# Two hand-written orders of one fused attention kernel: key and value weights on another DMA queue, all five engines' orders replaced

## The chip, the cores and the metric

The kernel runs on one core of a Trainium2 chip. The core has five engines that run side by side: TensorE (PE in the profile, with PEld for its weight loads), VectorE (DVE), ScalarE (ACT), GpSimd (POOL) and SyncE (SP), which here only issues DMAs. ScalarE issues DMAs on a queue of its own too. The metric is the time of one execution in microseconds on the device, the median of three runs.

## The reference

Thirty-two sequences `x` of 64 tokens with 256 features attend to a context `ctx` of the same shape, in four blocks, one after the other; everything is float32:

```
x = L0(x, ctx)   # whole-slab normalisation, 8 heads of 64 channels attending over the 256 feature columns, residual
x = L1(x, ctx)   # layer norm of the context, 16 heads of 16, key mask, gated (tanh) residual
x = L2(ctx, x)   # queries from x, keys and values from context and x together, key mask, RMS norm, MLP of 1024, residual
x = L3(x, ctx)   # self attention, cross attention, MLP of 1024, each behind a layer norm, with residuals
```

All four need softmax over masked scores. The weights are loaded once; activations of a pair of sequences stay on the chip from the first block to the last.

## The kernel before, in words

The 32 sequences are worked on as 16 pairs (a pair fills the 128 partitions). The work on a pair is cut into stages, each with a letter: `n` normalises `x` for L0 and makes its values from the context, `q` its queries, `a` scores and softmax (eight units of two 512-column score banks), `d` transposes the probabilities, multiplies them with the values and adds the residual; `k` does what depends on the context alone (keys and values of L1, L2 and L3's cross attention); `b` is L1, `e` L2's attention, `g` L2's MLP, `c` L3's self attention, `f` its cross attention, `h` its MLP. `s` is the setup (weights loaded and combined once), `w` are matmuls without use on a constant tile, `y` is the store.

For each stage and pair there is a Python generator for each engine that takes part, such as `act_n(i)` or `pe_a(i)`; it issues a few instructions between two `yield`s. What an engine issues next is set by a string in `ORDER`, one letter for one step of that stage's generator, which `weave` (line 207) walks through. So each engine is strictly in order, stages of several pairs are interleaved, and what is not fixed by the strings is done by semaphores: an instruction waits for what it reads and for the buffer that it writes. PSUM is used as seven rotating banks; `BANK` says which bank each fill takes, and an eighth bank (`attended`) collects the output of `d`, and of the `w` matmuls. A planner outside the program wrote `ORDER` and `BANK` from costs that it gives to each step.

The setup on PE (`pe_s`, line 1261) has seven steps: transpose the query and key weights of L0 (line 1268, its copy out of PSUM is line 1327 on VectorE); multiply them into one matrix per head ("m", lines 1276 and 1279; it waits for the two loads `cols` and `bv_raw`, which share one semaphore); multiply value and output weights ("wvo", line 1286); a bias ("bias", line 1293); three rows of bias (line 1301). The first `WARM_UP` of the `w` matmuls (line 1235) stand at the start, the rest near the end, behind the last pair's L0 residual.

The first steps of PE and SyncE, decoded from the strings (a number is the pair; x00, x01: transposed probabilities; att: attended matmuls; v0, v1 of `n`: line 433; q: line 510; a: line 539; k1: line 659):

```
PE: w x13, wT, n0.mean, k0.cT, m, wvo, bias, k0.nT, n0.var, n0.v0, k0.k1, q0 q0, a0.0, n0.v1, a0.1, k0.v1, k0.k2, row1,
    k0.v2, d0.x00, a0.2, a0.3, n1.mean, ...
SP: x of pair 0, context of pair 0 for k, cols+bv, context of pair 0 for a (cc), q0+o0 of wb, rows, residual, context of pair 1 for k,
    q1+o1, x of pair 1 (waits for q0), w1+w2, masks, ...
```

ScalarE issues seven setup loads first (`act_s`, line 1308): two halves of L0's query and key weights, its value and output weights, and three 512 KB loads of key and value weights (kv0 and kv1 of `wb`, kv1 of `wc`).

Of the kernel before, what the change touches and what calls it, by code (L numbers as in the profile page):

```python
# [62 lines left out]
WARM_UP = 13  # L63
IDLE_WORK = 62
# [18 lines left out]
def transpose_fills():  # L83
    fills = []
    for u, j, n in units():
# [24 lines left out]
        "nksnssdksnsebssnfsndnkebbndfnknfnedenybbbkfndnkydenkebdnfbnyffdnnyebyeknkbednfnynkkdbddnefenyfnkyyfbnedfnykbkn"  # L110
        "enbfykebdnenbdefkynffydyyy"),
    "pe": (
        "wwwwwwwwwwwwwsnksssknnkqqanakkskdaanddkdddaadddsdnsddaddddaqddqaadkdddkkddnanaddbkbdndbdddaaddbdbddbaabkeddnee"
        "dededdddddqqaaddeekbeennaedbekkbagndddggggddbdbaabdcdbcecncecdddaacdeecdddcdcedqqafddddfddfeeeennaefddfebfbkkf"
        "kaagkdggndggbdddkhkkchcckbchhbhacbdddnbaddaedcedcedacdecedddfdddfqqfddeebeeannefbefafdkfdkkaagkkgghkkdgnghdkhd"
        "dbaddchncdchdbbccabdddbdaaeccedcdeceeddqqfdddfdfddeeeenanebffafekkkbfaagkkgdghgdgkknhhbdhdchckccbbddacbnddddba"
        "ddaaecceecdddcdeeddfddddfqqfddeeeebnanefbefaaafgkgkkfgkdkggbdkhnkdhchdcckbchhddacddbddbnddaaacdbcdedcedeceeddf"
        "dddfdqfddeebeeqanebfefanafdkkfkadnkgkkggbdhgghhkbcdhcccbhddcaabddkdbndcddecdaaceeddcdeeqddfdddfdddfeeeeqnaneff"
        "afbebkkfkaadkgkkdgngkhgddgkbddchhccchhacbddbddnbaddcbddecaacdeedceeddqdfdddfddfeeeebaqnanefbfafekkdkfddkgdnkgg"
        "ggbddaadhdkkckdccdhbcnhbddcabdhdbchecaacedecdeedddfdddfqfddeeeennqaefbfefbkfkkaaagkdghghdnhbdgngkkkkhchcdcbcbd"  # L120
        "dcabddddbaddecdecdaacedcededdfdddfdqfddeeeenqaeffnafekkabkfbdkkgkdggbadgdgkhnddbkchchdcbchhacbdddnbaddaaecceed"
        "ddcdeceqdddfdddfddfeeeeaqnneaffebfbkkkfagkdgdghdggbadkhhcnkbcchbhccddbkddaadbdckcneddaacdeeecdddeqdddfdddfddfe"
        "eeenqanebffeafbkfkgkdaadgkgdghngbdhkcnhckccddcabdkddhbhdbckddaaacbceddeecddeeddqfddddfddfeeeebnaqebffeanfdkdkf"
        "gaakgngkggdbhdkkhchbcccddcdnbdhaabhkddbkcceddaaceddedcdeeddfddddfqqddfebeeebnaefnfefkkfkaaagkkgdghkgkhdgbdhdkc"
        "hccchcddbbdaabdccddbcddecdaaefdefdfdeedddddfdfdfkkkfdkebekbeewbehkehhgbbgbgbgegeeewwweckcchcwwwwwwwceeeehecwec"
        "wwwckgcggfggfwwfwwwwcwwwcccffcwfkfwwwcwwwcwwwcwhchwwfhfwwfhhwfwwfwwwfwwwwfwwwwwwwwwwhwwwhhhh"),
# [12 lines left out]
    "dve": (
        "nknsnknknnsksnsnnnsnknananaaknassaaandaadnakknnaaaadanadsannkenbaakdndaasaaakadaadanaaandnaaankdndbbbbnbanbbaa"  # L140
        "bndbdbbabaaabaabaanaennedndaeeneeeeddaeaedaekbanaennaaeaegagggkbgnbbbnknadbdgagbkbbfgcbbabbcencaacbdbaacnancec"
        "cdccaccaacnccnccebncadaacndcffaefeeefeeaddfaeffefafefenffnffeffdfkaeagkgfngggafaakhgnahdgdaahnbegcbbccnnhcbbbb"
        "bnabhbkbcbkhckhafcaccbddncacaacbccacaadcennccneaaackdncafffeefeedefdkefffedefefefaffafeffnfeagaagfkngfagbghane"
        "hahkanhdgaggnhcccdahckbknbbnabkabnadbbcncbbdbnbhbkakccccancbccanbccadcacfcanceedcffaaafeeeafeeedfdffeffffeefef"
        "ndnfffefaakefagagafgggaafhkahahaghgandngcnkbhncnchcnbbdbbbbbcbakbhcbbbaccccbaddcbcaacaccenaccacaenneanacdacndf"
        "fefeafeeeddfekkeefffdkefffefaffaenffegagfaggangaakfafhggbkhaahnhngbbbakcbccbencbnhbbbdhnbbdkafccbhacncaccdcdcc"
        "akncaakbcncaacbcadaanncenedacffefeafeeedfkedffedfffeeeffaaffebnfaefgafkaggnngafnafagnhkhaaknhafghdbbgbbbbgbcnb"
        "chbccbhebcdacnbcchaccaccbdacacdnabcccncnaanaknaaeckeacdkffdefaeefeeedkdfeffefeffefffaffnffadeaaanfkaegggnfgaag"
        "afanbahhgdhkhgkndgccbccbbbkbabbbnbhnbcbbhnchaccccadcdkccacabnabcaneccnacadkaaecaedncafnfefeeefkededfedfbefeffe"
        "faafffnnfefaffaakfeaggaggnngdfankgndegagbhhchbnccbabhcabdabkaacbfbnbdkbahbcnhbcnccncaccbckancbacdhcccaanaaceea"  # L150
        "cffkfdafeeeeeedfdeffkefedfffefnffffefankafegagbgnfnhghaahgakahaaaghdnnnghbnbgbcbcckekbcbbabbcnbfdkchbabccackcc"
        "bdncadcbackabnaccnccaenadaceaacfaffdeeafeeedfedfffefeefefffafnffekdfanegggafgaafghkaaadekggfbbnhbbbbhnbhdbgncc"
        "ccnbaakbabchhncabnhaccccbandcdbaaaccckaacaccecnannekdnacdacfkeefafeefededfeeffeffefdafffanfeffnfaaegakgfggabgn"
        "afkhahhhgdgegbbbbcccnbbdcfbhnhcbcabbkbnanbahcccccacccbcacandaabccdnaakanknaaacaneneabcffddeekfeefeeddfefffefef"
        "dnffefafeffakefngaggafggkefhanahaahagankdghnnagcnaccnbcbbbbbdhbckbfbcnhcccbcnbnabcdcaccdcccahcbaakaabnacnaaeae"
        "dcfadfefeefeebeddfeefdfffefefaafffefkfkefgaagggnnkafgnkfnaahhaahngghadnkagcbbbcbeckbcbhnbdbbhbacbbncccccancadn"
        "ccabhcnabcadcckcfanaacnaeaaedcfdkafbfeefeeedkefdeedffefeefefkffffefffaeaggfknngfagaagkahahhaghgakaahgccbbcdacb"
        "bhkkbbdbcecbbbbcchckccbcccacabdcccbadacfbacfaffaafeaadefaffffakdfeffeffeffdfekefdeedeekeefhehhbbhbbebbeggegbgb"
        "gbkhbbbgbgbgceccfecheeeeeceeceececececccccecccecgggggcckffhfgfggfcccffcfffffcfcffffccccfcccfcccchcfhhhccffffhh"
        "ffffffffffffhfffhhhhhhh"),  # L160
# [99 lines left out]
def build(nc, dram, out):  # L260
    ctx = ExitStack()
    with ctx:
# [20 lines left out]
        wb = sb("wb", [P, WCOLS])  # L283
        wc = sb("wc", [P, WCOLS])
# [1075 lines left out]
        def sp_s():  # L1360
            sp = nc.sync
# [185 lines left out]
```

## Time and profile before

| | us |
|---|---|
| median of three runs (1220.17 to 1222.36) | 1220.33 |
| the profiled execution | 1221.77 |
| its span, from the first to the last instruction | 1220.0 |
| PE busy | 1189.9 |
| DVE busy | 958.0 |
| ACT busy | 848.0 |
| POOL busy | 614.0 |

A span is shorter than its execution's time by what lies before the first and after the last instruction, here 1.77 us. In the rows below, a line such as L539 is that line of the kernel; `out<-in` are the program's tile names; `x26` counts instructions (a float32 matmul is two of them); PEclk is the granted clock of TensorE, 1.00 for 2.4 GHz and 0.50 for 1.2 GHz.

### The profile page before, as it was taken

The page shows a single profiled execution, that of the slowest core. Times are in us where ns is not written, and L with a number is a line of the kernel's source. Part 1 is how long each engine was busy: PE and PEld are TensorE (multiplying, and loading weights), DVE is VectorE, ACT ScalarE, POOL GpSimd, SP SyncE. Part 2 cuts the span into 40 slices and gives each one's busy share as a digit, 9 for nine tenths or more (in the row PEclk, how much of TensorE's full clock was granted, in tenths as well). Part 3 has the DMA queues.
Part 4 walks back from the last instruction along what each step waited for, and adds up shares of the span by engine and source line. Part 5 has one row for each costly group of instructions (what it writes and reads, how often), then busy time and mean ns, then how long its engine had stood idle before and what let it go on. Part 6 is the DMA issues. An engine that isn't in the chain of part 4 may idle for free.

```text
span 1220.0 us, 35295 instructions
## 1 busy us (share of the span) xinstructions
PE 1189.9 (98%) x13174; PEld 974.5 (80%) x13174; DVE 958.0 (79%) x2298; ACT 848.0 (70%) x2275; POOL 614.0 (50%) x1003
## 2 busy tenths in 40 slices
PE   8999999999999999999999999999999999999998
PEld 7778787787887878788787887878787787877877
DVE  3778886969788797787969788697887969789764
ACT  2877676787867668686776667677686777866543
POOL 2653663637455473644646456373654645363341
PEclk7999999999999999999999999999999999999999
DMA  6501000000000000010100100000000000000000
GB/s 207 192 3 28 2 27 2 16 20 25 15 6 12 22 14 12 12 30 1 29 15 2 32 2 20 17 16 2 25 12 17 24 8 16 2 12 2 2 6 10
DMA packets 27623, 27.91 MB, mean 23 GB/s; under 512 B 11072, under 2 KB 25408, under 8 KB 26816
## 3 DMA queue, kind: packets, MB, share of 16 engines
q1 hardware_dynamic: 25808, 23.42, 6.3%
q10 hardware_dynamic: 1648, 2.23, 0.6%
q8 instruction: 109, 1.79, 0.6%
q14 instruction: 58, 0.48, 0.1%
HBM read 23.53 MB, written 2.10 MB: 21 GB/s over the span
## 4 chain that ended last, share of the span: by engine, by line
PE 75%; DVE 11%; issue 4%; POOL 4%; ACT 4%; DMA 1%; SPq 0%; POOLq 0%; DVEq 0%; ACTq 0%
PE bank L932 9%; PE bank L659 9%; PE bank L942 8%; PE bank L539 7%; PE attended L614 7%; PE bank L599 7%; PE bank L665 5%; PE bank L694 4%; PE bank L720 4%; PE bank L683 3%; PE bank L707 3%; PE bank L652 2%; PE bank L510 2%; ACT p_a L575 2%; DVE nmax_a L554 2%
## 5 line engine op out<-in xcount | busy, mean ns | idle before, releaser
L586 POOL TENSOR_SCALAR p_a<-p_a,rec_a 128x256 f32<-128x256 f32 x512 | 248.6, 502 | 116.3 <-DVE rec_a L560 116.3
L575 ACT ACTIVATE p_a<-bank,nmax_a 128x256 f32<-128x256 f32 x512 | 237.9, 475 | 57.3 <-DVE nmax_a L554 55.8
L554 DVE TENSOR_REDUCE nmax_a<-bank 128x2 f32<-128x512 f32 x256 | 170.7, 680 | 25.7 <-PE bank L539 25.3
L599 PE MATMUL bank<-ident,p_a 128*128 128x128 f32 x1024 | 143.7, 275 | 2.6 <-POOL p_a L586 1.4
L539 PE MATMUL bank<-cc,q_a 64*128 64x256 f32 x1024 | 133.9, 392 | 1.5 <-DVE p_a L632 0.3
L599 PEld LDWEIGHTS bank<-ident,p_a 128*128 128x128 f32 x1024 | 115.8, 141 | 19.6 <-issue 11.8
L614 PE MATMUL attended<-p_a,v_a 128*64 128x256 f32 x1024 | 125.2, 386 | 0.1
L539 PEld LDWEIGHTS bank<-cc,q_a 64*128 64x128 f32 x1024 | 93.6, 186 | 32.4 <-issue 19.4
L575 ACT ACTIVATION_READ_ACCUMULATOR p_a<-bank,nmax_a 128x1 f32 x512 | 105.1, 205 | 0.0
L614 PEld LDWEIGHTS attended<-p_a,v_a 128*64 128x64 f32 x1024 | 67.0, 136 | 44.0 <-issue 12.0
L632 DVE COPY p_a<-bank 128x512 f32<-128x512 f32 x128 | 86.4, 680 | 8.0 <-PE bank L599 7.9
L647 ACT ACTIVATE p_a<-bank 128x512 f32<-128x512 f32 x128 | 75.5, 600 | 15.5 <-PE bank L599 14.7
L932 PE MATMUL bank<-h_xnT,wc 128*128 128x128 f32 x512 | 62.0, 276 | 0.2 <-ACT h_xnT L887 0.2
L932 PE MATMUL bank<-g_xnT,wb 128*128 128x128 f32 x512 | 61.7, 276 | 0.0
L932 PEld LDWEIGHTS bank<-h_xnT,wc 128*128 128x128 f32 x512 | 59.7, 192 | 1.1 <-ACT h_xnT L887 0.7
L932 PEld LDWEIGHTS bank<-g_xnT,wb 128*128 128x128 f32 x512 | 59.5, 192 | 1.0 <-ACT g_xnT L887 0.4
L942 PE MATMUL bank<-wc,h_hid 128*128 128x256 f32 x256 | 59.8, 380 | 0.0
L942 PE MATMUL bank<-wb,g_hid 128*128 128x256 f32 x256 | 59.5, 380 | 0.0
L522 ACT ACTIVATE q_a<-bank,bq 128x512 f32<-128x512 f32 x64 | 41.9, 689 | 23.7 <-PE bank L510 23.6
L1116 POOL TENSOR_TENSOR e_p<-e_p,e_max 128x1024 f32<-128x1024 f32 x26 | 49.1, 1903 | 13.0 <-DVE e_max L749 12.7
L813 POOL TENSOR_TENSOR c_p<-c_p,self_add 128x512 f32<-128x512 f32 x32 | 40.4, 1273 | 23.2 <-DVE c_p L1150 23.2
L813 POOL TENSOR_TENSOR f_p<-f_p,m_add 128x512 f32<-128x512 f32 x32 | 40.5, 1274 | 22.9 <-DVE f_p L1199 22.9
(265 smaller groups left out, 2890.6 us busy)
## 6 DMA issues: line engine op xcount, KB each, us to landing
xx<-in_x SPq DMA_DIRECT2D x32, 128.0 KB, 2.8
cc<-in_ctx SPq DMA_DIRECT2D x32, 128.0 KB, 2.9
wc<-in_wc SPq DMA_DIRECT2D x3, 1024.0 KB, 11.5
k_c<-in_ctx SPq DMA_DIRECT2D x16, 128.0 KB
res_a<-in_x SPq DMA_DIRECT2D x16, 128.0 KB, 2.3
wb<-in_wb SPq DMA_DIRECT2D x2, 1024.0 KB, 6.2
out<-y_out SPq DMA_DIRECT2D x16, 128.0 KB, 2.2
wb<-in_wb ACTq DMA_DIRECT2D x2, 512.0 KB, 6.6
```

What stands on the lines that cost most here:

```text
L539: ins = mm(bs[e][:, qt * D:(qt + 1) * D], q_a[rows_, j, n, qt * P:(qt + 1) * P], cc[rows_, z, n, :], start=True, stop=True)
L554: dve.tensor_reduce(nmax_a[:, n, e, :], ps[:, :].rearrange("p (q k) -> p q k", q=KT), AX.X, ALU.max, negate=True).then_inc(A.s["max"], 1)
L575: last = act.activation(p_a[:, j % 2, n, e, qt, :], ps[:, qt * D:(qt + 1) * D], ACT.Exp, bias=nmax_a[:, n, e, qt:qt + 1], accum_out=sum_a[ ...
L586: last = pool.tensor_scalar(p_a[:, j % 2, n, e, qt, :], p_a[:, j % 2, n, e, qt, :], rec_a[:, n, e, qt:qt + 1], 1.0, ALU.mult, ALU.mult)
L599: last = nc.tensor.transpose(ps[:, kt * D + qt * P:kt * D + (qt + 1) * P], p_a[:, j % 2, n, e, qt, kt * P:(kt + 1) * P], ident[:, :])
L614: last = mm(attended_bank[n * S:(n + 1) * S, 0:D], v_a[:, n, kt, h * S:(h + 1) * S], p_a[:, j % 2, n, e, kt, :], start=h == 0 and kt == 0, ...
L632: release(A, dve.tensor_copy(p_a[:, j % 2, n, 1, :, :], ps[:, :].rearrange("p (k q) -> p k q", k=KT)), i, ("x", u, 1))
L647: release(A, act.activation(p_a[:, j % 2, n, 0, :, :], ps[:, :].rearrange("p (k q) -> p k q", k=KT), ACT.Copy), i, ("x", u, 0))
L659: last = mm(ps[:, m * P:(m + 1) * P], w[:, k, m * P:(m + 1) * P], srcT[:, k, :], start=k == 0, stop=k == KT - 1)
L813: pool.tensor_tensor(v, v, bc(mask_add[:, :], 1, HB), ALU.add).then_inc(T.s["madd"], 1)
L932: last = mm(ps[:, m * P:(m + 1) * P], W["w1"][:, k, cols_], T.xnT[:, k, :], start=k == 0, stop=k == KT - 1)
L942: last = mm(ps[:, 0:D], T.hid[:, m, :], W["w2"][:, m, :], start=m == 0, stop=m == MT - 1)
```

## The change

Three 512 KB weight loads leave ScalarE's setup and become three steps of SyncE's, right behind `cols` and `bv_raw` in the generator. `WARM_UP` goes from 13 to 17, `IDLE_WORK` from 62 to 63. `ORDER` and `BANK` are replaced for all engines; in the planner that wrote them, VectorE and GpSimd were taken to exclude each other. Apart from the `w` matmuls and the three loads, each engine's string holds as many steps of every stage as before.

```diff
-WARM_UP = 13
-IDLE_WORK = 62
+WARM_UP = 17
+IDLE_WORK = 63
...
     "sp": (
-        "nksnssdksnsebssnfsndnkebbndfnknfnedenybbbkfndnkydenkebdnfbnyffdnnyebyeknkbednfnynkkdbddnefenyfnkyyfbnedfnykbkn"
...
+        "nkssebsnsssnsnksdfkssdennsdnbbkdefndnnnebynkfnfybkbedenbkfdydnnfkdeyenbfnyknfdnbkynenefnddfykebknybbnnfeekfbny"
...
     "pe": (
-        "wwwwwwwwwwwwwsnksssknnkqqanakkskdaanddkdddaadddsdnsddaddddaqddqaadkdddkkddnanaddbkbdndbdddaaddbdbddbaabkeddnee"
...
+        "wwwwwwwwwwwwwwwwskwnsnksqqnanakkksaadskddkdnddadnsddsdaddaaddddqddqaaddkdkdkddnanabddkbddbdddnaaddbdbddbaanbdd"
...
     "act": (
-        "skknsqqqaankaaqdaadaakaaddaaadadaqqaqqadadkkakanaabdnabdadbabdabbaabaaedakdaeddqqqeaeaeqebeenaaneadbakggdgbbaa"
...
+        "skkqqqqnsaakaandaadaakaddaaaaddaqaaqqqaaddkaaknkaabnadbdadbabdabbabaaaekdadaedqqdqeaeaebeeenqaaendbaagdbggbkaa"
...
     "dve": (
-        "nknsnknknnsksnsnnnsnknananaaknassaaandaadnakknnaaaadanadsannkenbaakdndaasaaakadaadanaaandnaaankdndbbbbnbanbbaa"
...
+        "nsnkknknnnknsnnnnsnanankakaansssaasadaadnabnnanaknsaddkaaansnaaannddkaaaakeaakddaaadnaaannaanadkdbbbbbbanbaabd"
...
     "pool": (
-        "ssknaaaakakaaaankaaaakaaaaaaaaaaabbaaaaenaaeaaeeakeeaaagagcabacbaekcccaanaagcceaffaaaeefkfeeaaffkgaahakhccbkba"
...
+        "ssknkaaaaakaaanaaaaakakaaaaaaaaaabbaaaneaeaaaaeeekagaekaagaacbcabacancacaeaacceaffaaaeekffeeaagffkgahkaakhccbca"
...
         def act_s():
...
-            load_weights(nc.scalar, wb, "kv0", "b_kv0")
-            load_weights(nc.scalar, wb, "kv1", "b_kv1")
-            load_weights(nc.scalar, wc, "kv1", "c_kv1")
...
         def sp_s():
...
                 sp.dma_start(dst, src).then_inc(setup["cols_in"], 16)
+            yield
+            load_weights(sp, wb, "kv0", "b_kv0")
+            yield
+            load_weights(sp, wb, "kv1", "b_kv1")
+            yield
+            load_weights(sp, wc, "kv1", "c_kv1")
             yield
             load_weights(sp, wb, "q0", "b_q0")
```

Decoded, the new strings start so:

```
PE: w x16, wT, k0.cT, w, n0.mean, m, n0.var, k0.nT, wvo, q0 q0, n0.v0, a0.0, n0.v1, a0.1, k0.k1, k0.v1, k0.k2, bias,
    a0.2, a0.3, d0.x00, row1, k0.v2, ...
SP: x of pair 0, context of pair 0 for k, cols+bv, kv0 of wb, four mask loads, kv1 of wb, context of pair 0 for a (cc), kv1 of wc,
    q0+o0, rows, x of pair 1 (waits for q0), q1+o1, contexts of pair 1, w1+w2, residual, ...
ACT: seven loads become four; k0.cT, k0.xnT, four q0, n0.v0, tanh, first exponentials, ...
DVE: statistics of x, copy of wT, second half of the statistics, context statistics, ...
```

## Rows read from the trace of the kernel before

**Rows 1.** The page's busy table: us, share of the span, instructions.

```profile
PE 1189.9 (98%) x13174; PEld 974.5 (80%) x13174; DVE 958.0 (79%) x2298; ACT 848.0 (70%) x2275; POOL 614.0 (50%) x1003
```

**Rows 2.** Windows: stretch, us, busy of PE/PEld/DVE/ACT/POOL, clock, DMA share, GB/s.

```profile
6.54:10.08 3.54, 1.23 (x10) 0.78 (x8) 2.58 (x12) 0.38 (x1) 0.46 (x1) 0.95 1.06 333
10.08:23.36 13.28, 13.28 (x104) 11.28 (x106) 5.11 (x19) 1.50 (x4) 0.83 (x2) 0.50 0.64 212
...
100.00:1100.00 1000.00, 985.24 (x11134) 806.22 (x11132) 807.04 (x1951) 727.72 (x1960) 529.91 (x855) 1.00 0.05 15
1100.00:1220.00 120.00, 109.30 (x1228) 93.95 (x1224) 83.37 (x179) 57.76 (x115) 37.90 (x54) 1.00 0.02 5
...
24.52:60.80 36.28, 35.71 (x266) 27.08 (x268) 27.36 (x69) 29.16 (x101) 20.38 (x40) 1.00 0.57 199
...
0.00:10.00 10.00, 6.72 (x34) 6.28 (x34) 2.58 (x12) 1.67 (x2) 4.31 (x18) 0.99 0.80 210
```

**Rows 3.** Chain of waits, first 130 us: start us, us, what.

```profile
3.62 6.42 DMA bv_raw<-in_bv
...
11.54 3.60 PE bank L1286 x16
15.14 1.80 PE bank L1293 x32
...
17.77 2.01 PE bank L433 x8
19.78 2.00 PE bank L659 x8
21.79 2.71 PE bank L510 x8
...
24.52 1.13 PE bank L539 x8
25.66 0.86 PE bank L433 x8
...
28.45 0.89 PE bank L659 x8
...
94.45 1.92 PE bank L510 x8
```

**Rows 4.** Timeline, 0 to 40 us: start us, us, engine, line, operation, tiles.

```profile
1.05 5.65 PE L1235 MATMUL attended<-mean_of_all 128*128 128x128 f32 x26 [1.05 <-POOL minus_half L1241]
...
8.41 0.66 DVE L1327 COPY c_p<-bank 128x512 f32<-128x512 f32 x1
...
18.12 0.71 POOL L498 TENSOR_TENSOR small_a<-small_a,minus_half 128x2 f32<-128x2 f32 x1 [7.91 <-DVE small_a L463]
...
19.39 0.23 DVE L474 TENSOR_SCALAR small_a<-small_a,cols 128x2 f32<-128x2 f32 x1
...
20.13 0.73 DVE L478 TENSOR_SCALAR xx<-xx,small_a 128x256 f32<-128x256 f32 x2
...
20.30 0.20 ACT L1320 ACTIVATE tanh_gate<-gate 128x1 f32<-128x1 f32 x1
...
27.10 2.43 SPq L1438 DMA_DIRECT2D m_raw<-in_mask  x4
```

**Rows 5.** DMA issues, first 24 us: tiles, queue, count, KB each, us to landing.

```profile
e_p<-in_rows SPq DMA_DIRECT2D x1, 640.0 KB, 9.8
...
cc<-in_ctx SPq DMA_DIRECT2D x2, 128.0 KB, 8.2
```

**Rows 6.** Groups of VectorE's instructions: busy us, mean ns, idle before.

```profile
L632 DVE COPY p_a<-bank 128x512 f32<-128x512 f32 x128 | 86.4, 680 | 8.0 <-PE bank L599 7.9
...
L754 DVE TENSOR_TENSOR f_p<-f_p,f_max 128x512 f32<-128x512 f32 x32 | 29.4, 919 | 0.4
...
L754 DVE TENSOR_TENSOR b_p<-b_p,b_max 128x512 f32<-128x512 f32 x32 | 22.0, 686 | 0.4
```

**Rows 7.** One of ScalarE's four groups of table loads (66 in all).

```profile
L959 ACT ACT_TABLE_LOAD x33 | 42.3, 1283 | 0.6
```

More of the change, by code:

```diff
@@ L115 @@
[L115 to L119, printed above, removed]
@@ new lines @@
+        "ekeedededdddddqqaddekbeeenanaedbebadkgkdgdgbggbdddaabndcdbcecenccdddaadceedcddcdcedqqafddddfddfeeeebannebffefd"
+        "kkkfaagkkkgddngkghdghbddckhhdbcccbhacbdddnbaddaaecceedcdddceeddfddddfqqfddeeebeananefbfedfdkkaakgfdkgggndgddba"
+        "dhkdkchncbbdchccabkhdbhekddcdcaaceddecdeeddfdddfdqqfddeeebenaaefnfefbkfkkdaagkkghkdgngdghbdhkchcchcbkbddacbddd"
+        "dnbaddaaeddeccecedcdeddqqfdddfdfddeeebeannebfefaaafgkgkdfkgdknghgkkhddbckkccchhhddacdbbdddnabddcbdcdeaacdeedce"
+        "eddfdddfdqfddeeebeaqnebffeaafdkkkfangkkggbhdgghnhdhcbkcdchcnbcddaabkdddbdkcecddaaceddecddeeddfdddfdqfddeeeenan"
@@ new lines @@
+    "dve": (
+        "nsnkknknnnknsnnnnsnanankakaansssaasadaadnabnnanaknsaddkaaansnaaannddkaaaakeaakddaaadnaaannaanadkdbbbbbbanbaabd"
+        "bdbbnabannabaanabnanaenedadnaeeeeededaaeedeeaknbaaaaenaegbgggbbgdabbbkbggdkbbabbgbanecacncacanfnbnbdkcaanceanc"
+        "cdcccacaacccneccanckdndacancffefaeeefeaeaddfefffdefeffefnaffefffaeakfggggefgbaannaaanhkkhgdnhghgcdhnccbbcbbbbk"
+        "babfhbccbbnkbaknhaccacbcddnacacbcacnacaccacenennaacdacfffdafeeeeededffefffdeefefaanffafkfeffaanegdgkfgagagbfan"
+        "gakgnhaadghcncahbnchbabbcbanbnbbnkhbbbcnbdchfccnccnbaacbdacckccheccnacaaecdaaekcffdaefkefaeeedfdeffffekdefeffe"
+        "afnffefafnekagagfbanfhhggaghnfahaagkgkangdahcbbccbbchbcnnbbcdahbbbebkbancccacbddancbacacccaancadncacaeeacnncff"
+        "kdkafeeefeeedfdefeffdfefaaeffnfefffegfgaagbgangnaaafnkgkfaghhnhhdagkcnackcnhcbbbbcbadfkbkhenbbhbbcbbacccacdcac"
+        "ndcanbacnccbcncanaadaaceedacfffaekefeeedfedfffedefkefaefffafefnffaeaakgggfagafagkahahnhbghgbbnabnfbbgbbcenchnc"
+        "dbhncbbcabcndbhkcncccaaccabcncdnabckndacccaaknacaeaedcfdffaeeafeeedfedfkfeffeefefnffafnffedfanknekfgggagaagfaa"
+        "kadkahhahfanghbdgbbbbbbbgckccbhcnbnbkahcbnbchaccaccdcdacancanbccanekcbnccadckbnaeedacfafaefeeafeeefdffdfafedee"
+        "ffffeanfnfafaefankfeggnggfagnaahkghnhnahgdngdcbbbbbafnbaccndbcakbabbnahcbchdabacncaccdcbcckcaccbcncakaehaaceea"
+        "cdafffeefeeedfedfffeefeffkfnfeffdffeaanekfnkggangggaafahhaakabhgghdnafakgncbbcbacdhbncbbbbbbbncbcnkhcccacbcadc"
+        "bkdccachnaaccncenaaaneaacedacfffdeefaeeedfedffkeffekfeffefffnffaenakdfegagbgaggnakfaaahfggbbhaabbhbhbengncnacn"
+        "bbhdbncbcakhkcbkcbdhkacccacdcdccbacaanbccccaanakbcnenaaeacdffdnefeeafeeefddffedefeffenfaffnafeffafaegagkfggagf"
+        "hnnakghanghhdgnbecbbaccbbnkacadhbbnbccfhnabbbbncccaccaccabdaanccncnbacdhkckaaecaeadcadfffefaeeeeefddeffedeffke"
+        "faaffkffaneffnfaeggggfbgaffnaahnhaannkgdahghkangccbncdbcbnbbbahbbkbbcnnbbchccaccaccccdncdneacbhkaackcaabakcdea"
+        "aeacfdffeekafeeedfedffefdfeefffeffaeffafneggaggfaankgaanffahgnaahghhankdgbcbccebncbbnbnbabbbbhbncchkbdcccaacca"
+        "bccaacbhknddccbnkcacaanncaekdaeacffafdeeeeefeeddfedefffefeffeffkffeffaaegfgkngfngaaaghhaaaakhggahagcbbbccfcbbd"
+        "hbbabbbbhckcbdccccacacccccbaachdecdbkbcakakcfffaafeaaadfekffdfaffeffeffeffefdedekdfeeekeefhehhbbhbbebbefggggbb"
+        "gbebbhhbgbkgbgcececceeeeecceeeccececeeckcccecccecgggggcchgfffgfgcccfcfffffcffcfffffcccccfccccfcchchfhhccffffhf"
+        "ffffhfffffffffhfhhhhhhh"),
@@ new lines @@
+    "pool": (
+        "ssknkaaaaakaaanaaaaakakaaaaaaaaaabbaaaneaeaaaaeeekagaekaagaacbcabacancacaeaacceaffaaeekffeeaagffkgahkaakhccbca"
+        "abaccaenaaaccaaeffaaeegffeekkafafgaakhaacahcnbbaccakcaaccaeaefagfaaeeffeekkffahghaaakcaacbacbaccnaaaegacckeaaf"
+        "afaeekffeefgfakaaahahcackacabcbcanacacakaeeaffaaeeffkkeefagfaghakahcccaabkbanccacacaeaaeaaffaaeeffekeffkgagaaa"
+        "hakhccacaabcbcnaaaaccekeaaffaaeegkfkfeeffaagahakhacancaacbbaaccakeccaaaeffaaeegffeekffkghaaahakacccnaababccaec"
+        "caaaaekaffaaeeffeegffkkgahakaahcacacbbakaccacncaeaaaefafgaaeekfkfeeffaagkaahhaccancaabbccaacacakeaaeffaaeegffe"
+        "eaaffkgakhhaakccanbaacbkccaccaeaaaeaffaaeeffeekkgffaghahkacacbcnbacakcaacacaaeaaefaaagfkffeeffkgahahaakcackcbb"
+        "aaccaccgaaaffaaeaeffaaffkkkhehegbbekgcecccceeccgffccffkcffcchcchffffffhh"),
@@ L186 @@
-    "2351042351042351604253")
+    "01234560125346012536454014503623613463450215064210365426452160345215641620356142504365204365120463546513426025"
+    "61561053260415326043215643251643250160413602451346143641560234154356315643015423560142106120614325061342534502"
+    "34650243162501260260412360241534651346153016530165021320143526430562341056236243621360432510432561045324563210"
+    "43562431032135421563402142051240265314021645365140635124035123463260153462016421650413625041632504321504163025"
@@ new lines @@
+    "14252456123560124325632542650243615024651243051260541206534120650354350413260413264056450164501465310462163016"
+    "53204140610451040506413052643056204132065324036241506312054263015360415320415324016540163254106351602536410264"
+    "10625325360245360214306523501324613025461354631561402356215326415360415364012540125346015216052163416231460250"
+    "23125301425301425630412650143502315406251346051236430463504613520436514026531645031456013241025302653023042160"
+    "34512634510210652361306415302153064326541326504625106345106341502361502361540236432640321546023153146531451602"
@@ new lines @@
+    "53160231501505246105246524126504312316251632510462510465213052413056246052604521603452412615206341520635024651"
+    "20312015243062413024135603240165312654132654013240362140316452014532605461046312546246024605324610563165312503"
+    "46251034625146504635406213521635412605412630415623150316423504162136251360513426056245641023502645126304123604"
+    "12360256023415605625032534620134620135426054126305420160140631254310610621520160654321605430636035210643521064"
+    "20346510246351063510623451062345264315205624301526052652463152406316523651243605142605146203514620351430435016"
@@ L189, in fill_places @@
+    "45302164156213546210435213201435261045312046532046531053416052346105304651320413240132640132645012364502136502"
+    "4163524163502416350216")
 def fill_places():
```

79 lines of the change are left out of this document (19 added, 60 removed).

## The prediction

> **What bounds the kernel now.** I read the busy table first, then the windows, then the chain of waits, and last the timeline of the first 25 us. The busy table says that TensorE (PE) is occupied for 98% of the span [rows 1]; since ends of matmuls are modelled, that alone proves little. The windows split it [rows 2]: in the body, from 100 to 1100 us, PE is idle for 1000 − 985.24 = 14.8 us, so no order of instructions can win more than about 15 us there. In the last 120 us it idles 10.7 us, although idle matmuls ("w") fill holes. The start is worse than its busy digits tell: from 10.08 to 23.36 us PE is busy without a break, but at granted clock 0.50, the 1.2 GHz level. Just before, from 6.54 to 10.08, it worked 1.23 of 3.54 us [rows 2]. The reader is to see the price in the chain: the same eight matmuls of line 659 take 2.00 us in that stretch and 0.89 us later, those of line 433 2.01 and 0.86 us [rows 3]. What ends the hole before it is the landing of the small bv vector, 6.42 us after its issue, at 10.04 [rows 3]. From the first scores (24.52) to 60.80, where the last attended matmuls of pair 0 begin, PE is busy 35.71 of 36.28 us [rows 2], so time won before 24.52 is carried on as long as the softmax engines follow, and the body behind it is bound by PE as well.
>
> All terms are differences against the profiled execution, 1221.77 us (span 1220.0 and 1.77 us around it). The median shown is 1220.33; I subtract from that.
>
> **The change part by part.**
>
> *Warm-up.* Sixteen "w" instead of 13 stand ahead of the first transposition, and one more behind the context's transposition. Each is two passes; 26 passes take 5.65 us from 1.05 on [rows 4]. The eight added ones cost 0.9 us at 0.11 us a pass (0.89 us for eight of the same 128x128 shape [rows 3]). They lie in the hole between 6.7 and 10.08 us, whose cover is the wait for bv, so I price them at 0; without that cover they would cost 0.9 us. The first transposition then ends near 7.6 us, and VectorE's 0.66 us copy of it [rows 4], which the new order puts ahead of the statistics' second half, ends near 8.6. So the mean matmul comes near 9, not 8.64, still ahead of bv.
>
> *Weights moved to SyncE's queue.* Three loads leave ScalarE's queue and stand behind cols and bv on SyncE's. Ahead of bv nothing is added; bv may land sooner than 10.04, but PE cannot use it before about 9.0 (the mean above). Bounds 0 and −1.0; I take 0. Behind bv the first attention context (cc) now waits for the issue of two weight loads and four mask loads. The masks took 2.43 us to issue [rows 4], the weights about 0.5 us each, so cc's second issue ends near 8.9 instead of 5.5. By bytes, 2.1 MB stand ahead of it on both queues, which is what 210 GB/s move in 10 us [rows 2]: it lands near 11. If it took its old 8.2 us [rows 5] it would land at 17.1, against a need near 15.6. I take the bytes, 0; the other end is +1.5. The rows load (bias rows) now lies behind more; ScalarE's tanh waits for it and precedes the first exponential. It ran at 20.30 with 6 us in hand [rows 4]. New: by bytes near 17, by its old 9.8 us [rows 5] from an issue near 10.5, 20.3. Need: about 17.5. So 0, other end +2.8. The second weights (w1, w2) and all later loads are freed earlier, since the wait of SyncE for pair 0's query matmuls ends earlier.
>
> *The order up to the first scores.* Old, from 10.08 to 24.52 us: 14.44 us. New, the 1.80 us of bias matmuls (line 1293) and the 2.00 us of the first key projection (line 659) stand behind the scores [rows 3]. That leaves 10.6 us at the old clock. If the clock stays at 2.4 GHz, these shrink: line 1286 3.60 to 1.8, line 433 2.01 to 0.86, line 510 2.71 to 1.92 [rows 3], the setup products 1.46 (10.08 to 11.54) to something between 0.73 and 1.46, the small rest 0.84 to 0.42. Sum 5.7 to 6.5. VectorE's chain to the normalised x then shows: variance, GpSimd's power 0.71, three small steps 0.8 (18.83 to 19.62), normalisation 0.73 [rows 4], about 2.5 us behind the variance matmul, 0.4 us later than line 1286 ends. So the first scores start between 16.2 and 16.9; I take 16.5, 8.0 us earlier. Still owed are bias (0.9 at the full clock) and key projection (0.89): 1.8 us. Net −6.2.
>
> *Body.* The work is the same: each engine's string has the same letters but for "w" and three SyncE loads. On PE the first projection of B follows pair attention more closely, the rest of the handovers stand at like distances; I counted PE work between producer and consumer for each kind and found some shorter and some longer. ScalarE's string changes function tables 68 times instead of 66: 2 x 1.28 us [rows 7], hidden in an engine that is 70% busy; without that cover +2.6. I take 0 for the body; bounds −14.8 (all PE idle gone) and, as the same size upwards, +14.8.
>
> *Tail.* One more idle matmul: 0.2 us, in holes; 0.
>
> Here the Trainium skill speaks against part of the change. Row first: subtracting the maximum takes 686 ns in B and 919 ns in F, with GpSimd at work beside it, but the copy out of PSUM of line 632 stays at 680 ns [rows 6]. The Trainium skill ("SBUF — State Buffer", section "SBUF: two separate sides") says that VectorE and GpSimd lock a shared port pair for whole instructions, but that VectorE takes part only with two SBUF inputs or in a two-port mode. The trace agrees. By the rule, taking the engines to exclude each other altogether keeps apart work that could overlap, so the sum would gain nothing in the body; by the row of F, undoing its stretch gives back 32 x 0.23 = 7.5 us of VectorE's time, if all of it reached PE.
>
> Sum: −6.2 + 0 + 0 = −6.2, so 1214.1 us.
>
> **The rivals.**
> *The clock falls again near 9.7 us.* For it: the small products at 10 us and the waits around them remain. Against: PE now has 0.9 us more of passes, and the context transposition in the hole. Then first scores come at 10.08 + 10.6 = 20.7, 3.8 us earlier; 2.6 us more at half clock cost 1.3, and 1.8 are owed: −0.7, 1219.6 us.
> *The body gains as well.* If half of PE's idle goes because stretches like F's 7.5 us are planned around: −6.2 − 7.4, 1206.7 us. Against it: waits in the body are short and spread over all lines.
> *Slower: results out of PSUM come late.* VectorE runs in order. If the new plan puts one eviction like line 632 (0.68 us [rows 6]) too late on a way for which PE waits, once for each of 16 pairs, that is +10.9: 1220.33 − 6.2 + 10.9 = 1225.0. It decides from 0.54 us a pair (8.6 in all), where the start's gain is used up and 0.2% more. For it: the plan sees exclusion where rows show none. Against: distances on PE are alike.
> *The change doesn't do what it says*: the context still lands late and pushes the first scores by 1.5 us; 1215.6, inside the forecast's own range.
>
> **How the numbers follow.** Forecast (clock stays, body within 3.5 us) 0.50; clock falls 0.22; body gains 0.10; slower 0.18. About 0.2% (2.4 us) is what can be told from no change: faster means below 1217.9, slower above 1222.8. The forecast, 1210.5 to 1217.6, is all faster. The clock rival, spread by 3 us of body, gives a third faster, half the same and the rest slower; the body rival is all faster; the slower rival one third the same. So faster 0.67, same 0.17, slower 0.16. The likeliest case alone: 1210.5 to 1217.6. The range that holds 8 in 10 reaches to the clock rival, most of the body rival and half of the slower one: 1207 to 1223.5.
>
> **What would show it.** Granted clock 1.0 from about 7 to 25 us, line 1286 taking near 1.8 us and the first line 539 near 16.5 us: right. Clock 0.50 in 10 to 23 us: the first rival. Line 433 waiting for cc, or the first exponential for tanh: the load terms were wrong. PE idle in 100 to 1100 us differing from 14.8 by over 4 us, or the body's steps drifting against the old times: the zero for the body was wrong. The work behind pair 0's last attended matmul not coming 6 us earlier though the first scores do: PE did not bind there.

## The result, and the profile after

The changed kernel takes 1199.34 us (median of 4 runs, 1198.61 to 1199.49), the kernel before on the same chip 1220.88 (4 runs, 1220.17 to 1222.36). The ratio is 0.982, 95% interval 0.980 to 0.984. I had forecast 1214.1 and a range of 1207.0 to 1223.5: the direction was right, but the gain of 21.5 us is three and a half times the forecast 6.2, and the time lies below the range.

The profiled execution after took 1199.37 us, span 1197.6. Busy table of the changed kernel:

```profile
PE 1178.5 (98%) x13184; PEld 974.1 (81%) x13184; DVE 942.7 (79%) x2298; ACT 849.1 (71%) x2277; POOL 608.6 (51%) x1003
```

Against [rows 1] VectorE (DVE) is busy 15.3 us less and GpSimd (POOL) 5.4 us less, for the same 2298 and 1003 instructions: they take less time each. The windows of the changed kernel (stretch; us; busy of PE, PEld, DVE, ACT, POOL; clock; DMA share; GB/s):

```profile
6.54:10.08 3.54, 2.10 (x43) 1.83 (x42) 2.48 (x11) 0.38 (x1) 0.23 (x1) 1.00 1.09 277
...
100.00:1100.00 1000.00, 992.53 (x11354) 819.32 (x11352) 812.28 (x1980) 737.49 (x1983) 531.16 (x865) 1.00 0.05 15
1100.00:1197.60 97.60, 90.35 (x979) 78.39 (x978) 60.82 (x143) 45.29 (x86) 30.04 (x41) 1.00 0.02 6
...
11.54:18.36 6.82, 6.82 (x27) 6.07 (x28) 2.36 (x8) 1.99 (x4) 0.23 (x1) 0.50 0.89 274
```

The row 100 to 1100 is the one to read twice. Its busy time rose by 7.3 us against [rows 2], but in the same 1000 us TensorE ran 11354 instructions instead of 11134: 220 more, 2.0%. So busy time alone does not tell how much work a stretch holds.

A mark for the stages is the issue of the last attended matmul (line 614) of a pair of sequences. The view of one line gives the first and last start in a window; here pairs 1 (first row, last start) and 15 (second row, last start), in the kernel before:

```profile
L614 PE MATMUL attended<-p_a,v_a x32: 379/379/430, 90.6 to 100.0; 128*64 128x256 f32 x32
...
L614 PE MATMUL attended<-p_a,v_a x64: 379/379/431, 1075.1 to 1110.3; 128*64 128x256 f32 x64
```

and in the changed kernel:

```profile
L614 PE MATMUL attended<-p_a,v_a x32: 379/379/431, 86.9 to 95.5; 128*64 128x256 f32 x32
...
L614 PE MATMUL attended<-p_a,v_a x48: 379/379/430, 1066.1 to 1088.2; 128*64 128x256 f32 x48
```

So the start gained 100.0 - 95.5 = 4.5 us; the body from pair 1 to pair 15 took 1010.3 us and takes 992.7, 17.6 less, some 1.25 us a pair; what lies behind took 1220.0 - 1110.3 = 109.7 and takes 109.4. Together 22.4 us, the difference of the spans. Between the two marks both kernels run the same number of TensorE instructions (no line's count differs by more than 8), here first before and then after:

```profile
100.00:1110.30 1010.30, 994.63 (x11226) 812.67 (x11222) 817.34 (x1967) 733.32 (x1974) 534.35 (x862) 1.00 0.05 15
```

```profile
95.50:1088.20 992.70, 985.50 (x11226) 813.39 (x11222) 804.50 (x1964) 733.11 (x1975) 529.77 (x862) 1.00 0.05 15
```

Of the 17.6 us, 8.5 were idle time of TensorE (15.7 against 7.2) and 9.1 lay inside its busy time, for 11226 instructions at the same clock. A busy time whose ends are modelled hides part of the waiting.

The start, in the changed kernel's chain of waits:

```profile
2.46 6.09 DMA k_c<-in_ctx
...
11.35 3.19 PE bank L1286 x15
14.54 3.73 PE bank L510 x8
18.27 0.97 PE bank L433 x8
19.24 0.86 PE bank L539 x8
...
21.83 1.09 PE bank L659 x8
...
24.67 1.02 PE bank L1293 x32
```

and its timeline:

```profile
12.61 0.73 DVE L478 TENSOR_SCALAR xx<-xx,small_a 128x256 f32<-128x256 f32 x2
...
18.89 1.21 PE L539 MATMUL bank<-cc,q_a 64*128 64x256 f32 x8
...
20.00 0.21 ACT L1317 ACTIVATE tanh_gate<-gate 128x1 f32<-128x1 f32 x1
```

bv no longer ends the first hole, the context tile k_c does, at 8.55 us. The clock stays at 1.0 until 11.54 (before: 9.70) and is at 0.50, the 1.2 GHz level, until 18.36 (before: 23.36). In that stretch line 510 pays 3.73 us, more than the 2.71 of [rows 3], where the clock came back before its end, and line 1286 3.19 for 15 records against 3.60 for 16; line 659, behind it, pays 1.09 instead of 2.00. First scores: 18.89 us instead of 24.52. The loads that answer to [rows 5], after (count, KB, median us to landing):

```profile
e_p<-in_rows SPq DMA_DIRECT2D x1, 640.0 KB, 6.7
...
cc<-in_ctx SPq DMA_DIRECT2D x4, 128.0 KB, 4.2
```

Two of these four context loads are pair 1's; the two of pair 0 took 4.8 and 5.3 us.

The groups that answer to [rows 6], after:

```profile
L632 DVE COPY p_a<-bank 128x512 f32<-128x512 f32 x128 | 86.3, 679 | 6.2 <-PE bank L599 5.5
L754 DVE TENSOR_TENSOR c_p<-c_p,c_max 128x512 f32<-128x512 f32 x32 | 23.1, 723 | 0.3
...
L754 DVE TENSOR_TENSOR f_p<-f_p,f_max 128x512 f32<-128x512 f32 x32 | 22.1, 690 | 0.5
```

F's subtraction lost nearly all of its stretch (919 to 690 ns; B's 686 is the yardstick), the copy out of PSUM stayed as it was, and C's went down from 781 ns before:

```profile
L754 DVE TENSOR_TENSOR c_p<-c_p,c_max 128x512 f32<-128x512 f32 x32 | 25.0, 781 | 0.4
```

### The profile page after: what moved, and what is told of

It reads as the page before. It is cut to its first block, busy times and chain, and to the rows that moved or that the text cites. A ratio compares the mean times of both kernels' runs of the same rounds, so it can differ in the third digit from the quotient of the medians.

```text
span 1197.6 us, 35319 instructions
## 1 busy us (share of the span) xinstructions
PE 1178.5 (98%) x13184; PEld 974.1 (81%) x13184; DVE 942.7 (79%) x2298; ACT 849.1 (71%) x2277; POOL 608.6 (51%) x1003
## 3 DMA queue, kind: packets, MB, share of 16 engines
q10 hardware_dynamic: 1216, 0.66, 0.3%
## 4 chain that ended last, share of the span: by engine, by line
PE 88%; DVE 4%; issue 3%; POOL 2%; ACT 2%; DMA 1%; SPq 0%; POOLq 0%; DVEq 0%; ACTq 0%
PE bank L659 10%; PE bank L539 9%; PE bank L932 9%; PE attended L614 9%; PE bank L942 9%; PE bank L599 9%; PE bank L694 6%; PE bank L665 5%; PE bank L720 4%; PE bank L683 4%; PE bank L707 4%; PE bank L652 3%; PE bank L510 2%; PE bank L433 2%; PE bank L711 2%
## 5 line engine op out<-in xcount | busy, mean ns | idle before, releaser
L586 POOL TENSOR_SCALAR p_a<-p_a,rec_a 128x256 f32<-128x256 f32 x512 | 245.9, 498 | 93.2 <-DVE rec_a L560 92.7
L942 PEld LDWEIGHTS bank<-wb,g_hid 128*128 128x128 f32 x256 | 47.0, 190 | 5.5
L942 PEld LDWEIGHTS bank<-wc,h_hid 128*128 128x128 f32 x256 | 46.6, 190 | 5.7
```

Of the source, the lines that this page charges most:

```text
L586: last = pool.tensor_scalar(p_a[:, j % 2, n, e, qt, :], p_a[:, j % 2, n, e, qt, :], rec_a[:, n, e, qt:qt + 1], 1.0, ALU.mult, ALU.mult)
L942: last = mm(ps[:, 0:D], T.hid[:, m, :], W["w2"][:, m, :], start=m == 0, stop=m == MT - 1)
```

## The experiments

All ran beside the kernel before (1221.1 to 1221.6 us by the set); medians are given. "Body" is the time between the two marks above.

**Which part of the order brings what.** Splices of the two orders: on every engine one order up to a time early in pair 1, then the other order for what is left. The three weight loads go with the start.

```
-ORDER[e] = old[e]
+ORDER[e] = new[e] up to 60 us + (old[e] without these steps)      # s1, s1b
+ORDER[e] = old[e] up to 63 us + (new[e] without these steps)      # s2
```

> On every engine the changed kernel's order up to 60 us, then the old order of what is left; loads of the key and value weights on SyncE as changed. In the traces the changed kernel leads by 4.1 us (at equal TensorE work) when pair 0's last attended matmuls are issued and by 21.7 us at pair 15's. Theory (the start and the body gain apart from each other): the lead of the start is kept and nothing is added, 1216 to 1217.5 us. Rival (the body gains because the loads and first pairs come earlier): near 1199 to 1204 us. Rival (the start's lead is given back to the softmax engines): 1219 to 1221 us.

> The mirror image: the old order and the old loads up to 63 us, then the changed order of what is left. Theory (the body's order gains 17.6 us by itself): 1203 to 1204.5 us. Rival (the body needs the new start): 1215 to 1221 us.

s1: 1219.87 us, the range of the rival in which the lead is given back. s2: 1207.74, outside both ranges. In both TensorE stood still once at the seam for a bank that exponentials still held (2.1 us in s1, 3.0 in s2), since the banks of one order met the fills of the other; in s2 the granted clock was 0.50 behind it, from 67.1 to 70.5 us. So s1 was repeated with the old body's banks renumbered.

> As s1_new_start_old_body, but the old body's seven banks are renumbered so that those that come free first at the seam are used first. In s1 TensorE stood 2.26 us at 59 us, for a bank that exponentials of the scores still held; up to there it led by 4.9 us. Theory (the lead of the start is kept by the old body): 1216.5 to 1218 us. Rival (the old body gives it back at another place): 1219.5 to 1221 us.

1216.92 us (ratio 0.997, 0.996 to 0.998), the theory's range: the start alone brings 4.4 us and keeps it. The marks of s1b:

```profile
L614 PE MATMUL attended<-p_a,v_a x32: 379/379/430, 86.0 to 95.4; 128*64 128x256 f32 x32
...
L614 PE MATMUL attended<-p_a,v_a x64: 379/379/430, 1070.5 to 1105.6; 128*64 128x256 f32 x64
```

and of s2:

```profile
L614 PE MATMUL attended<-p_a,v_a x32: 379/379/430, 95.2 to 103.7; 128*64 128x256 f32 x32
...
L614 PE MATMUL attended<-p_a,v_a x64: 379/379/431, 1059.8 to 1096.2; 128*64 128x256 f32 x64
```

Body 1010.2 us with the old order and 992.5 with the new, whatever start stands ahead of it. The 17.6 us belong to the body's order alone.

**The stretch taken away.** An instruction's stretch is what it takes longer beside another engine's instructions than its kind takes otherwise (F's 919 ns against B's 686). Reductions of about the same length, with one SBUF input, take the place of the stretched instructions; v leaves out the subtraction of the maximum in B, C and F, v2 the normalisations as well. In both kernels:

```
-dve.tensor_tensor(v, v, max, ALU.subtract)                     # B, C, F
+dve.tensor_reduce(unused, v, AX.XY, ALU.max)                   # v, v2
-dve.tensor_scalar(T.xn, src, ...)  and the same for xx         # lines 857, 859, 478
+dve.tensor_reduce(T.xn, src in groups of one, AX.X, ALU.max)   # v2 only
```

> The kernel before, with the subtraction of the maximum in stages B, C and F left out on VectorE: in its place stands a reduction over the same 512 elements into an unused tile, with one SBUF input and the same waits (0.63 to 0.67 us in line 749, hardly stretched, against 0.686, 0.781 and 0.919 us in B, C and F). It takes about 12 us of stretch off VectorE, without touching any order. Theory A (the body gains because VectorE is no longer stretched beside GpSimd): 1206 to 1213 us. Theory B (it gains by where the steps stand, and the stretch is a by-product): 1217 to 1221 us.

> The same edit in the changed kernel, where the three subtractions take 0.68 to 0.72 us, so that only 1 to 3 us of VectorE's time go. Both theories: 1197.5 to 1199.5 us. Theory A wants the old kernel to gain over 7 us more by the edit than this one does; theory B wants both to gain alike within 2 us.

> The kernel before with the edit of v_old_no_stretch (1213.9 us) and, besides, each normalisation of a tile by VectorE (lines 478, 857, 859) replaced by a reduction over groups of one element, which copies the tile and leaves it unnormalised. Their stretch, near 10 us in all in the old trace, goes if such a reduction is not stretched by GpSimd. Theory A (stretch explains the whole of the body's gain): 1206 to 1210 us. Theory C (half of it; the rest is room on TensorE): 1212 to 1214 us.

> The same edit in the changed kernel (with the first half of it alone: 1197.1 us), where the normalisations are stretched by some 4 us in all. Both theories: 1195.5 to 1197.5 us; what counts is the difference to the old kernel with the edit: below 12 us by theory A, 14 to 17 us by theory C.

v: old 1213.87 (0.994 of before), new 1197.09: the old kernel gains 5.0 us more by the edit than the new, where theory A asked for over 7 and theory B for under 2. v2: old 1209.20 (0.990), new 1196.62: the old kernel comes into theory A's range, but the two stay 12.6 us apart, between A's 12 and C's 14. By the marks the body's gap between the orders shrinks from 17.6 to 12.1 us (1004.2 against 992.1) and then to 8.8 (1000.3 against 991.5). So half of the body's gain is the stretch, which theory A wanted whole and theory B not at all; the times say the same, 12.6 us between the orders with v2's edit against 21.5 without. What stretch is left can hardly pay the other half: between the marks VectorE is busy 801.4 us in v2's old kernel and 799.0 in its new one, where 817.3 and 804.5 stood, and GpSimd 516.7 and 515.2. Of the 8.8 us that remain, 3.5 are idle time of TensorE and 5.3 lie in its busy time. The same in the row 100 to 1100, first v's old kernel:

```profile
100.00:1100.00 1000.00, 988.12 (x11176) 810.06 (x11176) 804.32 (x1962) 729.43 (x1966) 519.72 (x862) 1.00 0.05 15
```

then v2's:

```profile
100.00:1100.00 1000.00, 990.12 (x11221) 812.51 (x11219) 801.19 (x1966) 730.91 (x1973) 516.65 (x862) 1.00 0.05 15
```

Beside PE's count (11134, 11176, 11221) look at the last busy figure: GpSimd, whose program was not touched, falls from 529.9 to 516.7 us. Its groups in the kernel before:

```profile
L586 POOL TENSOR_SCALAR p_a<-p_a,rec_a 128x256 f32<-128x256 f32 x512 | 248.6, 502 | 116.3 <-DVE rec_a L560 116.3
...
L824 POOL COPY e_qT<-e_rec 128x128 f32<-128x128 f32 x32 | 13.4, 439 | 6.7 <-DVE e_rec L761 6.7
```

and in v2's old kernel:

```profile
L586 POOL TENSOR_SCALAR p_a<-p_a,rec_a 128x256 f32<-128x256 f32 x512 | 237.4, 482 | 120.3 <-DVE rec_a L560 120.2
...
L824 POOL COPY e_qT<-e_rec 128x128 f32<-128x128 f32 x32 | 8.7, 294 | 5.0 <-DVE e_rec L761 4.8
```

The stretch is mutual: GpSimd's instructions are held up by VectorE's as well. The longest of the 512 products took 1.03 us before and 0.56 in v2.

**Time added to VectorE.** Is it VectorE's own longer time that costs, or the hold on GpSimd? First plain time ahead of F's 32 subtractions:

```
+if T is F: dve.tensor_reduce(unused, 160 elements of cols, AX.X, ALU.max)
```

> The changed kernel with a reduction over 160 elements (estimated at 0.23 us from 680 ns for 512) into an unused tile ahead of each of the 32 subtractions of stage F on VectorE, about the time by which these were stretched in the kernel before (0.919 - 0.686 us); 7.5 us in all. Theory D (VectorE's time costs TensorE the same in either order, about half of it): 1202 to 1204 us. Theory E (the new order leaves VectorE more room): 1199 to 1201 us.

> The same 7.5 us added to the kernel before, on top of its stretch. Theory D: 3 to 5 us more than before, 1224 to 1226 us. Theory E (the old order has the less room): more than that, and more than a_new adds to the changed kernel by over 2 us. Rival (TensorE doesn't wait for stage F at all): 1221 us.

New 1202.57 us, 3.2 over the changed kernel; old 1222.49, 1.2 over before (ratio 1.001, 1.000 to 1.002). Theory D holds for the new kernel and is missed by the old one; theory E wanted the difference the other way. But the same edit did not add the same time. F's subtractions, first in the old kernel with the edit and then in the new:

```profile
L755 DVE TENSOR_TENSOR f_p<-f_p,f_max 128x512 f32<-128x512 f32 x32 | 26.0, 813 | 0.0
```

```profile
L755 DVE TENSOR_TENSOR f_p<-f_p,f_max 128x512 f32<-128x512 f32 x32 | 23.1, 723 | 0.0
```

In the old kernel the added reductions draw off stretch (919 to 813 ns), in the new there was none to draw off (690 to 723). VectorE's busy time rose by 3.1 us in the old (958.0 to 961.1) and by 7.4 in the new (942.7 to 950.1). For each of these microseconds both pay about 0.4 us, and with times known to about 1 us these runs don't show which order has more room. Then a whole instruction of 512 elements ahead of each subtraction, in the old order:

```
+dve.tensor_reduce(unused, v, AX.XY, ALU.max)          # p: reads SBUF
+dve.tensor_tensor(v, v, max, ALU.subtract)            # l: the subtraction twice
+dve.wait_ge(twice, ...)                               # p, l: what was added is waited for
```

> The kernel before with a reduction over the tile's 512 elements (one SBUF input, 0.63 to 0.67 us) ahead of each of the 32 subtractions of stage F on VectorE, which waits for it: some 22 us more on VectorE. The 7.5 us of a_old_added_time cost 1.2 us. Both theories: 1224 to 1231 us; it is the standard for the next.

> As p_old_plain_time, but what stands ahead of the subtraction is the same subtraction once more (two SBUF inputs; the softmax doesn't change by it). Theory L (the price of such an instruction is that VectorE and GpSimd hold each other up: GpSimd's products of line 586 become late as well): over 4 us above p_old_plain_time, and the products' stretch, 13.3 us in the old trace, grows by 5 us or more. Theory T (only VectorE's own longer time counts, 0.05 to 0.29 us for each of the 32): 0.3 to 3 us above p_old_plain_time.

p 1238.02 us, above the 1224 to 1231 of both theories: 16.5 over before, for 15.9 us more of VectorE's busy time (958.0 to 973.9; the reductions take 21.8, but the subtractions behind them fall from 919 to 750 ns). l 1245.55, another 7.5. The added groups, first p's and then l's:

```profile
L755 DVE TENSOR_REDUCE unused<-f_p 128x8 f32<-128x512 f32 x32 | 21.8, 680 | 0.4
```

```profile
L755 DVE TENSOR_TENSOR f_p<-f_p,f_max 128x512 f32<-128x512 f32 x32 | 29.0, 906 | 0.4
```

l's added groups are 7.2 us longer than p's; VectorE's busy time is 6.0 us longer (973.9 to 979.9). At p's price (16.5 / 15.9, about 1.0 us for each us) that is 6.2 of the 7.5, and by the intervals (p 1.012 to 1.016 of before, l 1.019 to 1.022) the 7.5 is known to 3 us only. The granted clock fell in both profiled runs as well, to 0.50 for 3.4 us near 1216 us in p, and in l for 3.4 us near 314 and for 6.8 and 3.4 us behind 1197, so a part of either price is the clock's. The 7.5 us lie in theory L's range (over 4) and not in theory T's (up to 3). GpSimd's side is there (busy 611.5 us in p, 619.7 in l), but not where theory L put it: the products of line 586 grew by 3 ns (503 to 506), the copies of e_qT from 397 to 570. So VectorE's own time can pay for most; whether the hold on GpSimd pays anything beside it stays open. The price is also no constant: about 0.4 us for each us of VectorE's busy time in a_old and a_new, about 1.0 in p.

**Room on TensorE alone.**

```
 PE order:  ... producer | late step | next step ...
+PE order:  ... producer | next step | late step ...       # at 27 places
```

> The kernel before with 27 pairs of neighbouring steps exchanged on TensorE between 95 and 1125 us: wherever a step there starts over 0.3 us late for its kind of handover, the next step of another stage goes ahead of it. Banks go with their fills; the other engines' orders are untouched. The 27 delays add up to 14.7 us in the profile. Theory C (the old order leaves too little room on TensorE between a producer and its consumer, at a few dozen places): 1209 to 1216 us. Theory A (the delays come from the time that VectorE's and GpSimd's instructions take beside each other, and the exchanged step waits as well): 1218 to 1221 us.

1238.01 us, 16.4 slower than before in its set: both theories missed. Its waits of TensorE, 100 to 1100 us (who waits, for whom; us in all, times, longest):

```profile
PE bank L599 <- POOL p_a L586: 2.5, 3, 1.2
PE bank L652 <- DVE f_yT L859: 2.0, 4, 0.9
PE bank L694 <- ACT c_p L782: 1.7, 1, 1.7
```

Between the marks the body takes 1025.2 us, 14.9 more, of which 28.1 are idle time of TensorE instead of 15.7. I take it that the steps moved ahead weren't ready either, and that the other engines, still in the old order, got their inputs later; no run shows this step by step. These 27 exchanges on one engine don't bring the gain. That none could isn't shown.

**The start's terms.**

```
-sp: "nksnssdksnse..."    kv loads on ScalarE
+sp: "nkssebsnsssn..."    kv loads on SyncE; pe, act, dve, pool as before     # m1
```

> The kernel before with SyncE's part of the change alone: the three loads on SyncE and its order up to 60 us, behind it the old order of what is left; all other engines, the banks and the number of idle matmuls as before. The prediction's term was 0, with bounds -1.0 (bv lands sooner) and +2.8 us (tanh late). Theory: 1220 to 1222 us. Rival (the earlier context and bv bring part of the start's gain): 1217 to 1220 us.

1220.78 us (ratio 0.9997, 0.999 to 1.001): nothing, as predicted. Its first scores start at 22.46 us, 2 us earlier than in the profile of before, but that is how the old start varies: a_old's and l_old's, untouched there, start at 22.7 and 22.6. Their mark of pair 1 comes at 98.1 us instead of 100.0.

```
-pe: w x16, s,      k w n s,      n k s,      q q ...
+pe: w x16, s, w x6, k w n s, w w, n k s,      q q ...     # w8
+pe: w x16, s, w x6, k w n s, w w, n k s, w x3, q q ...     # w11
+pe: w x16, s, w n w w w s n k w s w w q q k ...           # w8n, with dve, act, pool to match
```

> The changed kernel with eight more idle matmuls (16 passes) on TensorE in the holes at 7.06 to 8.69 us (six) and 10.05 to 10.91 us (two). In the changed kernel's trace the clock falls to 0.50 at 11.54 and is back at 18.36 us, and the first scores start at 18.89. Theory (it falls because TensorE stands idle in these holes, and the start's lead is carried on): granted clock 1.0 throughout, line 1286 near 1.8 us instead of 3.2, first scores at 16 to 17 us, 1196.5 to 1198 us. Rival (the clock falls all the same): 1199 to 1200.5 us, first scores near 19. Rival (scores come earlier, but the softmax engines don't follow): first scores near 16.5 and yet 1199 us.

> w8_fill_the_holes with three more idle matmuls (six passes, 0.66 us) in its last hole of the start, 12.65 to 13.42 us, ahead of the first query matmuls, which wait there for the normalised input. Of w8's four runs two had clock 1.0 (1196.6 and 1197.1 us) and two 0.997 (1199.1 and 1199.6). Theory (that hole is where the clock can still fall): all runs at clock 1.0, 1196.4 to 1197.3 us. Rival (it falls by the holes before): the same two kinds of run as w8, median 1197 to 1199.5 us.

> w8_fill_the_holes, with the input's statistics ahead of the weights' copy on VectorE, ahead of the context's steps on VectorE, GpSimd and TensorE, and the transposition of the normalised context behind the first query matmuls (six more idle matmuls than the changed kernel instead of eight). Theory (the chain from the input's landing to the normalised input sets the first scores): first scores near 15 us instead of 16.07, clock 1.0, 1195.5 to 1197 us. Rival (the chain is no longer what comes last): first scores near 16, 1197.5 to 1199 us.

w8: 1198.10 us (1196.60 to 1199.61), its profiled run at clock 1.0 throughout. TensorE's start there:

```profile
10.81 2.00 PE L1286 MATMUL bank<-p_a 64*128 64x64 f32 x16
13.42 1.99 PE L510 MATMUL bank<-xx,wm 64*128 64x512 f32 x8 [0.61 <-DVE xx L478]
...
16.07 1.06 PE L539 MATMUL bank<-cc,q_a 64*128 64x256 f32 x8
```

First scores at 16.07 us, and pair 1's mark at 93.1 instead of 95.5: where the clock holds, 2.4 us more are won and kept. ScalarE in the same run:

```profile
16.90 0.61 ACT L490 ACTIVATE v_a<-bank 128x512 f32<-128x512 f32 x1
19.48 0.20 ACT L1317 ACTIVATE tanh_gate<-gate 128x1 f32<-128x1 f32 x1 [1.97 <-DMA self_mul<-in_self_mask]
19.59 0.46 ACT L575 ACTIVATE p_a<-bank,nmax_a 128x256 f32<-128x256 f32 x1
```

It stands 1.97 us ahead of tanh, whose semaphore counts four loads (rows, gate and two self masks), until the last has landed, and the first exponential starts 3.5 us behind the first scores; in the changed kernel it starts 2.0 us behind them (20.87 and 18.89). The full clock held in two runs (1196.6, 1197.1), in the other two the mean clock was 0.997 (1199.1, 1199.6). w11: 1198.72 (1196.99 to 1199.71); only one of four runs kept the clock at 1.0, and in the profiled one it fell at 13.68. So filling the last hole doesn't keep it, which holes matter stays open, and no version here holds the clock in every run. w8n: 1200.35 (1197.95 to 1203.67), above both ranges, first scores at 19.06: its value matmuls waited 2.13 us for a bank that the context's transposition held until ScalarE had scaled it, behind four query tiles. w8 is the fastest complete kernel by its median, by 0.1%, which its runs don't separate from the changed kernel.

## Why the prediction was wrong, step by step

- *Warm-up, 0.* Right as a price: the added passes lie in the wait for the landings, now k_c's (8.55 us), and the mean matmul came at 9.16, forecast near 9. The price of a pass, 0.11 us, does not fit the row it stands beside (26 in 5.65 us are 0.22 each), but it did no harm: the 32 passes ahead of the first transposition took 5.57. That they would keep the clock was not borne out.
- *Weights moved, 0.* Right for the kernel as it is: m1 shows no cost, and tanh ran at 20.00, before the first exponential. Going by bytes came nearer than the old durations: pair 0's context loads took about 5.1 us to landing where [rows 5] has 8.2, the rows' 6.7 where it has 9.8. But tanh's need of 17.5 us was not met. The sum let it wait for the rows alone, which landed near 17.6; its semaphore counts three more loads, the last issued 1.6 us behind the rows. In w8, where the clock held, the first exponential came some 1.5 us late by it: there the term was not 0.
- *Order up to the first scores, -6.2.* It gave 4.5 (marks) or 4.4 (s1b, by the medians); against the earlier of the old kernel's starts, with pair 1's mark at 98.1, it is 2.6. The sum presumed the full clock. The clock fell at 11.54 us, 1.84 us later than before, and first scores came at 18.89, between the forecast's 16.5 and the 20.7 of the rival in which it falls again. Where it held, in w8, they came at 16.07 and pair 1's mark 6.9 us earlier: the sum came out there, but its condition mostly wasn't met.
- *Body, "I take 0".* This step failed, by 17.6 us; s1b and s2 show that the body's order alone brings them. Two readings misled me. The bound of 14.8 us took PE's idle time for all that could be won; but of the 17.6 us only 8.5 were idle time, and 9.1 lay inside the busy time, for the same number of instructions. And I compared the PE work between producers and consumers, found it alike, and left it at that, with the stretch in sight in [rows 6]: I priced F's alone, at 7.5 us of VectorE's time, on VectorE's side alone, and put nothing of it into the sum. B, C, F and the normalisations with GpSimd's share in it are worth 8.8 us of the gap between the two bodies. The other 8.8 us stay open: r_old's exchanges of TensorE's steps alone didn't bring them, and which of the other orders does wasn't tried.
- *The rule on the shared port.* The Trainium skill ("SBUF — State Buffer", section "SBUF: two separate sides") says that the two engines lock a port pair for a whole instruction, VectorE only with two SBUF inputs or in a two-port mode. The trace agrees on which instructions take part (F's subtraction 919 and 690 ns in the two orders, the copy out of PSUM 680 and 679). I took from it that planning for exclusion keeps apart work that could overlap, and the trace does not agree with this use: the new order has as much overlap of the two engines from 100 to 1100 us as the old (507 us against 503, added up from both traces over each pair of instructions), but F's subtractions lie beside GpSimd for 8.5 us instead of 19.4 in the whole run. What was moved apart is what collides.
- *Table loads and tail, 0.* Right: 109.4 us behind pair 15's mark against 109.7.
- *The rivals.* "The body gains as well" had the mechanism, a chance of 0.10 and 1206.7 us; it was sized by half of PE's idle time. Its sign came true: PE's idle time from 100 to 1100 us went from 14.8 to 7.5 us. "Results out of PSUM come late" did not happen: line 632's idle time fell from 8.0 to 6.2 us.

## What to carry to other kernels

Don't take TensorE's idle time for the most that a better order can win. Between two marks that hold the same work in both orders, compare the whole time and not the busy share: here over half of the gain lay in time that counted as busy. If the same instruction has different mean times in different stages, price the difference on both engines that it involves, over all groups that show it. Cutting two traces at a mark that recurs in every stage says in which stage a difference arises, and splicing the two orders at such a mark shows whether stages are independent.

## What the runs showed of the hardware

- VectorE's subtractions and normalisations between SBUF tiles and GpSimd's instructions lengthen each other; reductions over the same tiles do so hardly. In v2's old kernel line 478's normalisation, as a reduction, takes 407 ns instead of 519, and GpSimd's products 482 instead of 502, its copies of e_qT 294 instead of 439.
- An instruction put ahead of a stretched one draws off part of its stretch: F's subtractions fell from 919 to 813 ns behind a reduction of 0.31 us (a_old), and to 750 behind one of 0.68 (p). So the time that an edit adds is read from the engine's busy time in all.
- The same program keeps or loses a part of TensorE's full clock from run to run: w8 has a mean granted clock of 1.0 in two runs and 0.997 in two, 2.5 us apart. In the changed kernel's profiled run, also at 0.997, it is lost between 11.54 and 18.36 us; where w8's two lost it no trace shows.
